# Mean, row scaling and copies of a layered kernel's norms move from VectorE to ScalarE, with a new order

## The reference

```python
def _layernorm(x, axis=-1, eps=1e-05):
    m = jnp.mean(x, axis=axis, keepdims=True)
    v = jnp.var(x, axis=axis, keepdims=True)
    return (x - m) / jnp.sqrt(v + eps)

x = x + _L0_attn_ref(_layernorm(x, axis=-1), ...)   # causal attention, 16 heads
x = x + _L0_ffn_ref(_layernorm(x, axis=-1), ...)    # 8 experts, top 2
x = x + _L1_attn_ref(_layernorm(x, axis=-1), ...)   # linear attention
x = x + _L1_ffn_ref(_layernorm(x, axis=-1), ...)    # 16 experts, top 1, and a shared one
x = x + _L2_attn_ref(_layernorm(x, axis=-1), ...)   # banded attention
x = x + _L2_ffn_ref(_layernorm(x, axis=-1), ...)    # 32 experts, top 4
x = x + _L3_attn_ref(_layernorm(x, axis=-1), ...)   # state-space layer
x = x + _L3_ffn_ref(_layernorm(x, axis=-1), ...)    # square of relu, then spikes counted
```

```python
def _rmsnorm(v, w, eps=1e-06):
    return v * lax.rsqrt(jnp.mean(v * v, axis=-1, keepdims=True) + eps) * w
u = _rmsnorm(x, norm1_w)
# ... a causal convolution over 4 tokens and a product give xh, then
xp = jnp.einsum('blhd,kd->blhk', xh, x_proj_w)        # dt_x, Bx (48 states), Cx (48 states)
dt = jax.nn.softplus(jnp.einsum('blhr,dr->blhd', dt_x, dt_proj_w) + dt_proj_b)
def step(h, inp):
    dt_t, b_t, c_t, u_t = inp
    a_bar = jnp.exp(dt_t[..., None] * A[None, :, None, :])
    h = a_bar * h + (dt_t * u_t)[..., None] * b_t[:, :, None, :]
    y_t = jnp.einsum('bhds,bhs->bhd', h, c_t)
    return (h, y_t)
# ... the outputs of all steps, through a product and a residual, then
h2 = _rmsnorm(x1, norm2_w)
mlp = jax.nn.silu(h2 @ gate_w.T) * (h2 @ up_w.T) @ down_w.T
```

## Time and profile before

| what | value |
|---|---|
| three runs | 1968.11, 1972.52, 1972.16 us; median 1972.16 us |
| the profiled execution | 1972.49 us, span 1970.7 us |
| instructions in it | 28714 |
| TensorE busy | 1636.1 us, 83% |
| VectorE busy | 1345.9 us, 68% |
| ScalarE busy | 918.5 us, 47% |
| GpSimd busy | 794.7 us, 40% |
| granted TensorE clock, mean | 0.903 of full speed |
| scans of layer 3 (L2028) | 384, 1204 ns each |

### The profile page before, as it was taken

How to read it: one execution, slowest core, us unless ns; L and a number is a source line. 1 busy time by engine, 2 the same in 40 slices (tenths; PEclk the granted TensorE clock), 3 DMA queues, 4 the chain that set the end, 5 groups by cost and what they waited for, 6 DMA issues and landing times.

```text
span 1970.7 us, 28714 instructions
## 1 busy us (share of the span) xinstructions
PE 1636.1 (83%) x10613; PEld 934.8 (47%) x10660; DVE 1345.9 (68%) x3025; ACT 918.5 (47%) x1623; POOL 794.7 (40%) x670
## 2 busy tenths in 40 slices
PE   7788889777787898966888989888778897988767
PEld 4456664323454676511355567542234565754104
DVE  5555567989555455899865555598985555559895
ACT  4354336544444443554445524445535453344543
POOL 2321125676133111587514221177742322127881
PEclk9899999877989998978899989898789998989779
DMA  6004402020000440211000053021100025111110
GB/s 213 1 1 135 136 6 70 28 71 27 11 1 2 138 134 9 65 61 53 11 11 1 22 160 95 17 76 47 45 11 6 1 62 168 47 38 55 57 35 11
DMA packets 91981, 105.41 MB, mean 53 GB/s; under 512 B 7104, under 2 KB 70336, under 8 KB 91584
## 3 DMA queue, kind: packets, MB, share of 16 engines
q1 hardware_dynamic: 89792, 99.37, 16.7%
q0 software_dynamic: 2048, 4.20, 0.7%
HBM read 80.60 MB, written 22.94 MB: 53 GB/s over the span
## 4 chain that ended last, share of the span: by engine, by line
PE 60%; DVE 19%; POOL 7%; ACT 7%; issue 6%; DMA 1%; SPq 0%; DVEq 0%; POOLq 0%; ACTq 0%
PE P L229 11%; DVE M L2028 6%; PE P L1643 5%; PE P L1874 5%; POOL M L2098 3%; PE P L1224 2%; PE P L1240 2%; PE P L969 2%; PE P L1821 2%; PE P L1229 2%; PE P L2156 1%; PE P L218 1%; PE P L1825 1%; PE P L1884 1%; PE P L397 1%
## 5 line engine op out<-in xcount | busy, mean ns | idle before, releaser
L2028 DVE TENSOR_TENSOR_SCAN M<-P,M 128x512 f32<-128x512 f32 x384 | 447.5, 1204 | 23.2 <-ACT P L1955 22.7
L1874 PE MATMUL P<-M,wt 32*32 32x512 f32 x3072 | 260.7, 747 | 134.4 <-DVE M L2028 81.4
L1955 ACT ACTIVATE P<-M,negA 128x512 f32<-128x512 f32 x384 | 262.6, 689 | 233.7 <-DVE M L2028 230.2
L229 PEld LDWEIGHTS P<-wt,M 128*128 128x128 f32 x2176 | 279.8, 196 | 101.4 <-issue 34.6
L229 PE MATMUL P<-wt,M 128*128 128x128 f32 x2176 | 295.0, 282 | 15.7 <-DVE M L1346 6.1
L2098 POOL TENSOR_TENSOR M<-M 128x512 f32<-128x512 f32 x192 | 240.3, 1283 | 125.6 <-DVE M L2013 89.9
L2098 POOL TENSOR_TENSOR M<-W,M 128x512 f32<-128x512 f32 x192 | 245.1, 1304 | 80.5 <-PE P L1874 80.2
L1874 PEld LDWEIGHTS P<-M,wt 32*32 32x32 f32 x3072 | 39.1, 114 | 285.8 <-DVE M L2028 176.7
L210 POOL TENSOR_TENSOR st<-st,wt 128x4 f32<-128x4 f32 x64 | 82.2, 1286 | 213.9 <-DVE st L193 211.9
L1643 PE MATMUL P<-M,wt 128*128 128x512 f32 x256 | 137.1, 618 | 2.0 <-ACT M L1692 1.4
L1740 DVE TENSOR_TENSOR M<-M,P 128x512 f32<-128x512 f32 x128 | 87.2, 682 | 69.7 <-PE P L1651 45.3
(11 more groups left out here) (350 smaller groups left out, 3221.2 us busy)
## 6 DMA issues: line engine op xcount, KB each, us to landing
W<-in_e SPq DMA_DIRECT2D x88, 192.0 KB, 2.7
M<-in_e SPq DMA_DIRECT2D x64, 192.0 KB, 2.7
M<-dt SPq DMA_DIRECT2D x48, 256.0 KB, 4.6
M<-xs SPq DMA_DIRECT2D x32, 256.0 KB, 3.1
ys<-M SPq DMA_DIRECT2D x32, 256.0 KB, 2.3
W<-du SPq DMA_DIRECT2D x32, 256.0 KB, 5.0
W<-xh SPq DMA_DIRECT2D x16, 256.0 KB
M<-du SPq DMA_DIRECT2D x16, 256.0 KB, 4.8
```

The costliest lines, as they stand in the source:

```text
L229: m = e.matmul(out[:, tok(j)], h[:, tok(j)], wgt, start=first and j == 0, stop=last, skip_group_check=True)
L1874: m = e.matmul(t["sums"][i // 2][to:to + 32, :], part("WC", c)[r, r], scan[r, :], start=c == 0, stop=c == 5, tile_position=(32 * i, to))
L1955: e.activation(t["aa"][n % 2][:, :], t["dtr"][i][:, :], EXP, scale=negA[:, c:c + 1]).then_inc(ACT.s, ACT.mark(b, "a3", "aa", n))
L2028: e.tensor_tensor_scan(bb[:, :], t["aa"][n % 2][:, :], bb[:, :], 0.0, MUL, ADD).then_inc(DVE.s, DVE.mark(b, "a3", "scan", n))
```

## The change

In all norms, ScalarE takes the mean off, in four pieces of 128 columns with the row's mean as its bias. It computes mean minus x, so the sign is turned, and the copy after the transpose turns it back (scale -1). Where layer 1's router uses the rows themselves, VectorE makes the sigmoid negative in the same instruction as before. VectorE no longer adds epsilon to the variance; GpSimd does that in front of its power. In layer 3, whose copy takes a gain, VectorE turns the sign of the mean (`neg`), and ScalarE adds it. The rows of both root-mean-square norms are scaled by ScalarE in four pieces instead of by VectorE in two halves; ScalarE adds the one to the exponential; and ScalarE copies the two spread inputs. The tables of turns are new for four engines, and two neighbouring bits have changed places in SyncE's.

```diff
@@ dve_norm
-            var = st[:, 24:32].rearrange("p (j c) -> p j c", c=2)[:, :, 1]
-            e.tensor_scalar(st[:, 32:36], var, 1e-5, None, ADD).then_inc(DVE.s, DVE.mark(b, tag, "var"))
             mean = st[:, 24:32].rearrange("p (j c) -> p j c", c=2)[:, :, 0]
-            e.tensor_tensor(v3(xk[:, :], 4), v3(x, 4), mean.unsqueeze(2).to_broadcast([128, 4, 128]), SUB).then_inc(
-                DVE.s, DVE.mark(b, tag, "xc"))
+            if tag == "a3":
+                e.tensor_scalar(st[:, 0:4], mean, -1.0, None, MUL).then_inc(DVE.s, DVE.mark(b, tag, "neg"))
             yield
             w.wait_ge(POOL.s, POOL.of(b, tag, "rstd"))
-            w.wait_ge(DVE.s, DVE.of(b, tag, "xc"))
+            w.wait_ge(ACT.s, ACT.of(b, tag, "xc"))
@@ pool_norm
-            w.wait_ge(DVE.s, DVE.of(b, tag, "var"))
+            w.wait_ge(DVE.s, DVE.of(b, tag, "mv"))
+            var = st[:, 24:32].rearrange("p (j c) -> p j c", c=2)[:, :, 1]
+            e.tensor_scalar(st[:, 32:36], var, 1e-5, None, ADD).then_inc(POOL.s, POOL.mark(b, tag, "var"))
+            yield
+            w.wait_ge(POOL.s, POOL.of(b, tag, "var"))
@@ act_norm
+            w.wait_ge(DVE.s, DVE.of(b, tag, "mv"))
+            for j in range(4):
+                e.activation(xk[:, tok(j)], x[:, tok(j)], IDN, bias=L.st[:, 24 + 2 * j:25 + 2 * j], scale=-1.0).then_inc(
+                    ACT.s, ACT.mark(b, tag, "xc"))
             yield
             w.wait_ge(PE.s, PE.of(b, tag, "xT"))
-            e.activation(dst, P[1][:, :], COPY).then_inc(ACT.s, ACT.mark(b, tag, "xn"))
+            e.activation(dst, P[1][:, :], COPY, scale=-1.0).then_inc(ACT.s, ACT.mark(b, tag, "xn"))
@@ dve_ffn1
-            e.tensor_scalar(sm[:, 168:172], sm[:, 168:172], 1.0, None, ADD).then_inc(DVE.s, DVE.mark(b, "f1", "e1"))
+            e.tensor_scalar(sm[:, 168:172], sm[:, 168:172], -1.0, -1.0, MUL, ADD).then_inc(DVE.s, DVE.mark(b, "f1", "e1"))
@@ dve_rms
-            w.wait_ge(POOL.s, POOL.of(b, tag, "rms"))
-            for i in range(2):
-                half = slice(256 * i, 256 * i + 256)
-                e.tensor_tensor(v3(y[:, half], 2), v3(rows[:, half], 2),
-                                st[:, 36 + 2 * i:38 + 2 * i].unsqueeze(2).to_broadcast([128, 2, 128]), MUL).then_inc(
-                    DVE.s, DVE.mark(b, tag, "y", i))
@@ act_rms
+            w.wait_ge(POOL.s, POOL.of(b, tag, "rms"))
+            for j in range(4):
+                e.activation(y[:, tok(j)], rows[:, tok(j)], COPY, scale=st[:, 36 + j:37 + j]).then_inc(
+                    ACT.s, ACT.mark(b, tag, "y", j))
@@ act_attn3
+            w.wait_ge(DVE.s, DVE.of(b, "a3", "neg"))
+            for j in range(4):
+                e.activation(T_[0][:, tok(j)], xt[b % 3][:, tok(j)], IDN, bias=L.st[:, j:j + 1]).then_inc(
+                    ACT.s, ACT.mark(b, "a3", "xc"))
...
+            w.wait_ge(ACT.s, ACT.of(b, "a3", "e"))
+            e.activation(T_[13][:, :], T_[12][:, :], IDN, bias=1.0).then_inc(ACT.s, ACT.mark(b, "a3", "w"))
...
+                w.wait_ge(PE.s, PE.of(b, "a3", "dub", i))
+                e.activation(t["dub"][i][:, :], P[2][:, :], COPY).then_inc(ACT.s, ACT.mark(b, "a3", "dub", i))
@@ dve_attn3
-            e.tensor_scalar(T_[13][:, :], T_[12][:, :], 1.0, None, ADD).then_inc(DVE.s, DVE.mark(b, "a3", "w"))
...
-            for i in range(2):
-                yield
-                w.wait_ge(PE.s, PE.of(b, "a3", "dub", i))
-                e.tensor_copy(t["dub"][i][:, :], P[2][:, :]).then_inc(DVE.s, DVE.mark(b, "a3", "dub", i))
@@ TURNS
             "sync": (191,
-                "400ffc003ffcc00ffc003ffcc00ffc003ffc801ff8007ffc"),
+                "400ffc003ffcc00ffc003ffcc00ffc003ffc801ff8007ffa"),
```

More of the change, by code:

```diff
@@ L1780, in pe_rms, with act_rms @@
                 yield
-                w.wait_ge(DVE.s, DVE.of(b, tag, "y", j // 2))
+                w.wait_ge(ACT.s, ACT.of(b, tag, "y", j))
                 e.transpose(P[1][:, tok(j)], y[:, tok(j)], ident).then_inc(PE.s, PE.mark(b, tag, "yT"))
-        def act_rms(e, w, b, tag, dst, gain):
-            P = lanes[b % 2].P
+        def act_rms(e, w, b, tag, rows, y, dst, gain):
+            P, st = lanes[b % 2].P, lanes[b % 2].st
+            yield
+            w.wait_ge(POOL.s, POOL.of(b, tag, "rms"))
+            for j in range(4):
+                e.activation(y[:, tok(j)], rows[:, tok(j)], COPY, scale=st[:, 36 + j:37 + j]).then_inc(
+                    ACT.s, ACT.mark(b, tag, "y", j))
             yield
@@ L1853, in pe_attn3 @@
                 if i:
-                    w.wait_ge(DVE.s, DVE.of(b, "a3", "dub", 0))
+                    w.wait_ge(ACT.s, ACT.of(b, "a3", "dub", 0))
                 else:
@@ L1865, in gather @@
                     w.wait_ge(ACT.s, ACT.of(b, "a3", "dtr", 1))
-                    w.wait_ge(DVE.s, DVE.of(b, "a3", "dub", 1))
+                    w.wait_ge(ACT.s, ACT.of(b, "a3", "dub", 1))
                 if k and c == 0:
@@ L1985, in dve_attn3 @@
             w.wait_ge(DVE.s, DVE.of(b, "a3", "rv"))
[L1986 removed]
+            dve_rms(e, w, b, "a3")
             yield
[L1988 to L1991 removed]
+            w.wait_ge(ACT.s, ACT.of(b, "a3", "w"))
             e.scalar_tensor_tensor(T_[12][:, :], T_[13][:, :], -1.0, T_[12][:, :], ADD, SUB).then_inc(
@@ L2052, in dve_attn3 @@
             w.wait_ge(DVE.s, DVE.of(b, "a3m", "mmv"))
-            yield from dve_rms(e, w, b, "a3m", x1, T_[XT - 1])
+            dve_rms(e, w, b, "a3m")
             for c in range(2):
@@ L2089, in inflow @@
                 if k == 0:
-                    w.wait_ge(DVE.s, DVE.of(b, "a3", "dub", q))
+                    w.wait_ge(ACT.s, ACT.of(b, "a3", "dub", q))
                 elif q == i:
```

65 lines of the change are left out of this document (33 added, 32 removed).

## The result

The changed kernel took 1916.24 us (four runs, 1911.35 to 1924.31) against 1972.34 for the kernel before in the same job: ratio 0.9738, 95% interval 0.9714 to 0.9762. By the medians the gain is 56 us, by the ratio 52 (47 to 56). The forecast was 1947 us with a range of 1917 to 1982. The profiled execution of the changed kernel is its fastest: 1911.35 us, 5 us under the median, at a mean granted clock of 0.935; the other three had 0.919 to 0.927.

A forecast was written before the change was run, and what follows sets the result against it. VectorE was taken to bound the four scan stretches (659.1 us), TensorE and hand-overs the other two thirds. Terms -31.7 - 17 + 9.3 + 10 + 4 = -25.4 from 1972.5 gave 1947 us, range 1917 to 1982.

The forecast's parts named there:

- Edits on VectorE, minus 31.7: In the four scan stretches, five removed kinds of VectorE work count in full, since VectorE is 92% busy there: -31.7 us.
- ScalarE's waits, plus 10: In the scan stretches and at lane hand-overs, ScalarE's added pieces hold back the scans' decay factors: +10 us, bounds 3 to 25.
- The order on VectorE, minus 17: The new table moves 46 other VectorE instructions out from between the scans, to where VectorE has free time: -17 us.
- more is won: Rival, 1922 us, chance 0.17: a third of VectorE's idle time in the stretches goes (-17), other work starts earlier outside (-8).
- TensorE's work moved outside, plus 9.3: Matmuls leaving the scan stretches, about 8 us, land outside where TensorE is 86% busy: +9.3 us, bounds 0 to 20.
- the order's terms: The two terms for the new order: VectorE work moved out of the stretches, -17 us, and its matmuls landing outside, +9.3.
- GpSimd and norms, plus 4: GpSimd's epsilon add lengthens the chain by 0.25 us in the 17 norms for which TensorE waits: +4 us.
- outside, I count nothing: Outside the scan stretches, 74.7 us of removed VectorE work counts as nothing: VectorE is 56% busy, the power covers the subtraction.
- the edits' terms: Three terms: VectorE work removed in the stretches, -31.7 us; scans waiting for ScalarE, +10; GpSimd's epsilon add, +4.
- A 128-column piece, 0.37: On ScalarE, one 128-column piece with a per-row operand takes 0.37 us, so a group of four takes 1.5 us.
- ScalarE is free at once: Condition in the norms: ScalarE's four pieces (1.5 us) lie beside GpSimd's add and power (0.3 + 1.38) if ScalarE can start immediately.
- The slower rival: Norms wait behind ScalarE's ordered queue, 0.85 us later over 56 norms, TensorE waiting 47 us more: 1994 us, chance 0.16.

The follow-up runs named there:

- two equally fast versions: Changed kernel without GpSimd's addition of epsilon, 1912.99 us; changed kernel with the addition of one and the spread-input copies back on VectorE, 1918.35 us.
- the spare instruction behind the scaling: Changed kernel plus one unused 512-column, one-input VectorE instruction behind the row scaling of each of 64 norms; 1936.26 us, ratio 0.9818.
- spare instruction of 0.26 us: Changed kernel plus one unused 4-column VectorE instruction behind the row scaling of each of 64 norms; 1933.07 us, ratio 0.9824.

## Why the prediction was wrong, by its own steps

- **Edits on VectorE, minus 31.7, and ScalarE's waits, plus 10.** Together -21.7 in the stretches; measured -24.6, by comparing the changed kernel with the old code in the new order. The sum was right and the parts were not: VectorE's busy time fell by 22.6 us and its idle time by 2.0. With the copies back nothing is lost, and over the whole change the scans wait 4.9 us less for ScalarE, not 10 more. That the two errors cancel is luck.
- **The order on VectorE, minus 17.** Measured -27.9. Of that 11.5 us is busy time moved out, where 17 stood, and 16.4 is idle time of VectorE that is gone, which the sum had at nothing. The rival "more is won" had that half as -17, and its 1922 was nearest; its second half, 8 us outside, was too small.
- **TensorE's work moved outside, plus 9.3.** The order alone costs 12.7 there by the profiles. Right within the error. Taken together the order's terms were -7.7, and the ratios give -8.
- **GpSimd and norms, plus 4, and "outside, I count nothing".** This is the step that failed. Of the edits' terms, -17.7 in sum, the ratios give -44. In the stretches only 3 us of the difference lie; the rest is outside, where the prediction had +4 and the profiles give -21.6 (19 when the 24.6 us of the stretches are taken from the 44, and 12 to 14 in the two equally fast versions). That is 16 to 26 of the 31 us by which the forecast missed. The +4 for the addition itself was of the right size; the nothing for the rest was not.
- **What stands in its place.** The edits pay outside, but only at their places in the queues: the same edits in the old order lose 28 us there, and ScalarE's pieces one turn later cost the whole gain. The norms themselves got shorter, not longer: 163.7 us in sum in the old code with the new order, 146.5 in the changed kernel. The power is 0.34 us shorter by the median, because no VectorE instruction stands beside it. The prediction took the 1.38 us of the earlier trace rows as the power's own time and read L195 as wholly beside it; 0.52 of its 0.69 us were. The trace of before had the shorter powers too (ns, min/median/max):

```profile
L210 POOL TENSOR_TENSOR st<-st,wt x64: 999/1382/1577, 7.4 to 1949.0; 128x4 f32<-128x4 f32 x64
```

But shorter norms don't explain the gain by themselves: TensorE's waits for scaled rows are 41.3 us in the old code with the new order and 39.6 in the changed kernel, and with the spare instruction behind the scaling, or the row scalings of the root-mean-square norms undone, the norms stay short and 16 to 33 us are lost. The clock takes part in it, with 14 us of doubled distances less; but that is a figure of the changed kernel's fastest execution. The prediction had the clock of 0.81 to 0.83 in the earlier trace rows and no term for it.

- **A 128-column piece, 0.37.** It took 0.387 (median). Right. "ScalarE is free at once" held in 46 of 64 norms, and the run with the pieces a turn later shows that the whole gain can be lost by this, a property of the table. The slower rival had its place right and decided from 0.45 us a norm; in that run the norms grew by 0.69 us each.

What stays open: how the 14 to 22 us outside come about, and what the 16 root-mean-square scalings pay for. A spare instruction of 0.26 us costs 17 us by the ratios, and no wait that I found is longer with it. Within one kernel the time goes with the clock: the changed kernel took 1911.35 us at 0.935 and 1924.31 at 0.919. But with the mean undone it took 1930.6 at 0.924, so the clock isn't the whole difference between kernels. That the saved VectorE time keeps the clock up, or that it hangs on where TensorE's short pauses fall, is not shown. None of the versions beats the changed kernel without leaving work out.

## What to carry to other kernels

Before taking an instruction's duration as its own, look at what ran beside it: GpSimd's power was a quarter shorter with VectorE's subtraction away. Where every engine's queue is ordered, do not price an edit at nothing because its engine is half idle: price the chain it stands in, and expect edits to pay only with the order that fits them. Give TensorE's clock a term of its own, from the distances of equal matmuls and not from the mean clock, and check it on more than one profile: executions of one kernel differed by 13 us with it.

## What the runs showed of the hardware

A GpSimd operation that starts beside a VectorE operation on SBUF ends only after it. The 4-element addition took 228 ns with nothing beside it, 455 beside VectorE's 427 ns with one input and 720 beside its 692 ns with two (medians); the power took 1037 alone and, with mean and subtraction back on VectorE:

```profile
L210 POOL TENSOR_TENSOR st<-st,wt x64: 1002/1381/1505, 7.6 to 1918.6; 128x4 f32<-128x4 f32 x64
```

The Trainium skill ("SBUF — State Buffer", "SBUF: two separate sides") says that GpSimd shares a pair of ports with a VectorE operation that has two SBUF inputs or runs in a 2-port mode, under an exclusive lock, and that the later one fully blocks. The traces agree but for its first part: behind the VectorE operation's end the addition took another 0.09 us of its 0.23 and the power 0.88 of its 1.04, so 0.14 to 0.16 us of each had run beside it. They show the same for the one-input addition; which mode it ran in they don't tell. The prediction had drawn from a like rule only that the addition would gain nothing where it goes, and left the power beside the subtraction out.
